# Tile codes for parts of two and three chunks of an edge group, in a one-core graph layer

## What is computed

```python
xn = layernorm(x)
sums   = segment_sum(xn[src], dst)            # 20,000 edges into 625 nodes
counts = segment_sum(1, dst)
gnn = (sums / max(counts, 1)) @ W_l.T + xn @ W_r.T + b_r
x = x + gnn + mixer(xn)                       # 8 heads, second-order attention
h = layernorm(x)
H = gelu(h @ W1 + b1)                         # 1024 wide
e = argmax(H @ Wg + bg)                       # one of 8 experts per node
x = x + prob[e] * (H @ Wd[e] + bd[e])
```

## Time and profile before

| | |
|---|---|
| median of 3 runs | 253.75 us (253.46 to 253.86) |
| the profiled execution: its own time | 254.01 us |
| its span in the profile | 252.3 us |
| TensorE busy | 236.2 us, 94% |
| VectorE busy | 148.1 us, 59% |
| ScalarE busy | 145.2 us, 58% |
| GpSimd busy | 31.8 us, 13% |
| granted TensorE clock | 0.995 of 2.4 GHz |

### The profile page before, as it was taken

The page is one execution under the profiler, slowest core; times in us unless marked ns, Lnnn a source line. Parts: engine busy times, 40 slices in busy tenths (PEclk is TensorE's granted clock), DMA queues, the critical chain, the costliest instruction groups (busy, mean ns, idle before and its releaser), DMA issues.

```text
span 252.3 us, 4726 instructions
## 1 busy us (share of the span) xinstructions
PE 236.2 (94%) x1428; PEld 149.6 (59%) x1429; DVE 148.1 (59%) x422; ACT 145.2 (58%) x223; POOL 31.8 (13%) x64
## 2 busy tenths in 40 slices
PE   7899999998798999999999999998899999999990
PEld 2448675664454553433368886574455578888880
DVE  2999999999999949961125557722800243223220
ACT  2878997999999956899960015444043323333000
POOL 7470000000000008300000000000450000000331
PEclk9999999999999999999999999999999999999997
DMA  6560000000000000099930000030033000000111
GB/s 232 189 216 3 1 3 3 5 4 3 3 5 0 5 3 3 0 370 421 416 130 4 0 0 0 9 131 25 26 84 105 0 1 3 0 1 3 36 34 33
DMA packets 6030, 15.82 MB, mean 63 GB/s; under 512 B 2724, under 2 KB 3783, under 8 KB 4723
## 3 DMA queue, kind: packets, MB, share of 16 engines
q1 hardware_dynamic: 4432, 12.64, 13.5%
q0 software_dynamic: 1280, 1.31, 2.0%
q10 hardware_dynamic: 288, 1.44, 1.4%
HBM read 14.08 MB, written 1.30 MB: 61 GB/s over the span
## 4 chain that ended last, share of the span: by engine, by line
PE 64%; ACT 21%; DVE 11%; issue 1%; POOL 1%; DVEq 0%; POOLq 0%
ACT mem L518 19%; PE ps L1270 16%; PE ps L1208 7%; PE ps L1090 7%; PE ps L1254 6%; PE ps L1111 5%; PE ps L1170 4%; DVE mem L722 4%; PE ps L1238 3%; PE ps L939 3%; DVE mem L725 2%; PE ps L1159 2%; PE ps L1161 2%; PE ps L967 1%; DVE qk_sb L768 1%
## 5 line engine op out<-in xcount | busy, mean ns | idle before, releaser
L518 ACT ACTIVATE mem<-ids_m,half_src 125x628 bf16<-125x628 f16 x96 | 69.7, 814 | 0.0
L722 DVE TENSOR_SCALAR mem<-node_ids,dst_f 125x628 bf16<-125x628 f16 x160 | 53.1, 387 | 0.0
L1004 PE MATMUL ps<-mem 125*128 125x501 bf16 x180 | 50.8, 374 | 0.4 <-issue 0.3
L1270 PE MATMUL ps<-mem 128*125 x192 | 41.6, 379 | 0.0
L1006 PE MATMUL ps<-mem 125*128 125x126 bf16 x180 | 39.3, 219 | 0.0
L1270 PEld LDWEIGHTS ps<-mem 128*125 128x125 f32 x192 | 36.0, 188 | 5.3
L616 ACT ACTIVATE qk_sb<-ps,sc_col 125x626 f32<-125x626 f32 (+1 forms) x40 | 28.6, 778 | 3.7 <-PE ps L1090 3.7
L1004 PEld LDWEIGHTS ps<-mem 125*128 x180 | 17.6, 98 | 20.4 <-issue 1.9
L725 DVE TENSOR_SCALAR mem<-ids_m,src_f 125x628 bf16<-125x628 f16 x64 | 25.0, 390 | 0.0
L665 ACT COPY mem<-mem 128x1000 f32 x8 | 8.2, 1031 | 19.8 <-PE ps L1270 19.8
L1090 PE MATMUL ps<-mem 32*125 32x313 f32 (+1 forms) x160 | 19.1, 472 | 0.2 <-DVE mem L795 0.2
(11 more groups left out here) (204 smaller groups left out, 281.0 us busy)
## 6 DMA issues: line engine op xcount, KB each, us to landing
mem<-in_wd SPq DMA_DIRECT2D x8, 1024.0 KB, 13.1
w_sb<-in_w SPq DMA_DIRECT2D x1, 1024.0 KB, 7.8
vz<-in_bd SPq DMA_DIRECT2D x1, 1000.0 KB
wqkv_sb<-in_w_qkv ACTq DMA_DIRECT2D x1, 768.0 KB, 6.4
x_all<-in_x ACTq DMA_DIRECT2D x1, 640.0 KB, 4.9
row<-rows_sorted SPq DMA_DIRECT2D x1, 579.7 KB
wlr_sb<-in_w_lr SPq DMA_DIRECT2D x1, 512.0 KB, 5.1
bqk_all<-in_b_qk SPq DMA_DIRECT2D x1, 256.0 KB, 4.2
```

Source lines behind the costliest of these rows:

```text
L518: ins = nc.scalar.activation(oh[:, g % OHB, 0, j, :], ids_m1[:, :], ACT.Sign, bias=half_src[:, g * GC + j:g * GC + j + 1])
L722: ins = nc.vector.tensor_scalar(oh[:, g % OHB, 1, j, :], node_ids[:, :], dst_f[:, col:col + 1], None, ALU.is_equal)
L1004: mm(psf[:, bass.ds(tile * BANK, TW + 1)], node_of, oh[:, buf, 0, j, 0:TW + 1], start=False, stop=False, skip_group_check=True)
L1270: ins = mm(ps[0:TP, 4 + n % EB, 0:C], hT_step[:, n % EB, k, :], wd_sb[:, bass.ds(e, 1), k, :], start=(k == 0), stop=(k == KH - 1))
```

## The change

Each group of five chunks gets two codes in place of one, for a part of its first two chunks and a part of the last three. A part's code has six bits: three for the first tile, two for the second tile less one, and one that is set (as the value 4 added to the two bits) for more than two. Four codes, those of a pair's two groups, go into one 24-bit number in float32 on GpSimd, and so into one integer. At a tile border only the part that has the border is repeated at the second tile. For this the sums of the signs are taken by part (weights 1.5 and 1, so that one threshold serves both), the small tables have 64 columns in place of 32, and GpSimd's chain up to `codes_ready` has 20 operations in place of 11. Each part's products have their own tile register and addresses. Two tables move into `mem`.

```diff
+    PARTS = ((0, 2), (2, GC))
+    NS = NG * len(PARTS)
...
-        PAIR = 256
+        PART = 64
+        PAIR = PART ** 4
+        OTHERS = sum((PART - 8) * PART ** s for s in range(4))
...
-            nc.gpsimd.memset(ones_col[:, :], 1.0)
+            nc.gpsimd.memset(part_col[:, 0:1], 1.5)
+            nc.gpsimd.memset(part_col[:, 1:2], 1.0)
...
             step(nc.gpsimd.tensor_tensor(span[:, :], last, first, ALU.subtract))
-            step(nc.gpsimd.tensor_scalar(two_code[:, :], span[:, :], 0.0, 8.0, ALU.is_gt, ALU.mult))
-            step(nc.gpsimd.tensor_scalar(more_code[:, :], span[:, :], 1.0, 128.0, ALU.is_gt, ALU.mult))
-            step(nc.gpsimd.tensor_tensor(two_code[:, :], two_code[:, :], last, ALU.mult))
-            step(nc.gpsimd.tensor_tensor(more_code[:, :], more_code[:, :], first, ALU.add))
+            step(nc.gpsimd.tensor_scalar(more_code[:, :], span[:, :], 1.0, 4.0, ALU.is_gt, ALU.mult))
+            step(nc.gpsimd.tensor_scalar(span[:, :], span[:, :], 0.0, None, ALU.is_gt))
+            step(nc.gpsimd.tensor_scalar(two_code[:, :], last, 2.0, 4.0, ALU.is_lt, ALU.mult))
+            step(nc.gpsimd.tensor_tensor(two_code[:, :], two_code[:, :], last, ALU.add))
+            step(nc.gpsimd.tensor_scalar(two_code[:, :], two_code[:, :], -1.0, None, ALU.add))
+            step(nc.gpsimd.tensor_tensor(two_code[:, :], two_code[:, :], span[:, :], ALU.mult))
             step(nc.gpsimd.tensor_tensor(two_code[:, :], two_code[:, :], more_code[:, :], ALU.add))
-            by_pair = two_code[:, :].rearrange("o (p w) -> o p w", w=2)
-            step(nc.gpsimd.tensor_scalar(pair_hi[:, :], by_pair[:, :, 1], float(PAIR), None, ALU.mult))
-            step(nc.gpsimd.tensor_tensor(pair_hi[:, :], pair_hi[:, :], by_pair[:, :, 0], ALU.add))
-            nc.gpsimd.tensor_copy(flags[:, :], pair_hi[:, :]).then_inc(codes_ready, 1)
+            step(nc.gpsimd.tensor_scalar(two_code[:, :], two_code[:, :], 8.0, None, ALU.mult))
+            step(nc.gpsimd.tensor_tensor(two_code[:, :], two_code[:, :], first, ALU.add))
+            by_pair = two_code[:, :].rearrange("o (p w) -> o p w", w=4)
+            step(nc.gpsimd.tensor_copy(pair_code[:, :], by_pair[:, :, 3]))
+            for s in (2, 1, 0):
+                step(nc.gpsimd.tensor_scalar(pair_code[:, :], pair_code[:, :], float(PART), None, ALU.mult))
+                step(nc.gpsimd.tensor_tensor(pair_code[:, :], pair_code[:, :], by_pair[:, :, s], ALU.add))
+            nc.gpsimd.tensor_copy(flags[:, :], pair_code[:, :]).then_inc(codes_ready, 1)
...
-            for j in range(GC):
-                ins = mm(ps[0:1, 0, 0:(T - 1) * NG], ones_col[:, :], ge[:, :, :, j], start=(j == 0), stop=(j == GC - 1))
+            part_sums = ps[0:1, 0, 0:(T - 1) * NS].rearrange("o (k g s) -> o k g s", k=T - 1, s=len(PARTS))
+            for s, (lo, hi) in enumerate(PARTS):
+                for j in range(lo, hi):
+                    ins = mm(part_sums[:, :, :, s], part_col[:, s:s + 1], ge[:, :, :, j], start=(j == lo),
+                             stop=(j == hi - 1))
...
-            def products(g, tile):
+            def products(g, s, tile):
                 buf = g % OHB
-                for j in range(GC):
+                lo, hi = PARTS[s]
+                for j in range(lo, hi):
...
-            def other_tiles(g, own):
+            def other_tiles(g, s, own):
                 with pe.If(own > 7):
-                    products(g, nc.s_assert_within((own >> 3) & 15, min_val=0, max_val=T - 1,
-                                                   skip_runtime_bounds_check_because="a second tile is there"))
-                    with pe.If(own > 127):
+                    products(g, s, nc.s_assert_within(((own >> 3) & 3) + 1, min_val=1, max_val=T - 1,
+                                                      skip_runtime_bounds_check_because="two bits and one"))
+                    with pe.If(own > 39):
...
             def pair(p):
                 code = codes[p]
-                for g, own in ((2 * p, code), (2 * p + 1, code >> 8)):
-                    first = nc.s_assert_within(own & 7, min_val=0, max_val=T - 1,
-                                               skip_runtime_bounds_check_because="each group has edges, each of a tile")
+                for g in (2 * p, 2 * p + 1):
                     pe.wait_ge(oh_ready, g + 1)
                     pe.wait_ge(steps_ready, g + 1)
-                    products(g, first)
-                with pe.If((code & 0xF8F8) > 0):
-                    other_tiles(2 * p, code & (PAIR - 1))
-                    other_tiles(2 * p + 1, code >> 8)
+                    for s in range(len(PARTS)):
+                        first = nc.s_assert_within((code >> 6 * (2 * (g - 2 * p) + s)) & 7, min_val=0, max_val=T - 1,
+                                                   skip_runtime_bounds_check_because="each part has edges, each of a tile")
+                        products(g, s, first)
+                with pe.If((code & OTHERS) > 0):
+                    for g in (2 * p, 2 * p + 1):
+                        for s in range(len(PARTS)):
+                            other_tiles(g, s, (code >> 6 * (2 * (g - 2 * p) + s)) & (PART - 1))
```

More of the change, by code:

```diff
@@ L83, in gps_layer @@
         BIG = 2 * KH * N
-        assert OH + 6 * N <= WD + BIG and T * (N + 1) <= WD
+        assert OH + 2 * T * NS + 6 * N <= WD + BIG and T * (N + 1) <= WD
         mem = sb("mem", [P, WD + BIG])
@@ L103, in gps_layer @@
         half_src = sb("half_src", [TP, NCH])
-        tile_of = sb("tile_of", [1, T, NG])
-        edge_tiles = sb("edge_tiles", [1, 2, T - 1, NG])
-        between = sb("between", [1, T, NG])
-        span = sb("span", [1, NG])
-        two_code = sb("two_code", [1, NG])
-        more_code = sb("more_code", [1, NG])
-        ones_col = sb("ones_col", [TP, 1], BF16)
-        pair_hi = sb("pair_hi", [1, NP])
+        edge_tiles = sb("edge_tiles", [1, 2, T - 1, NS])
+        span = sb("span", [1, NS])
+        two_code = sb("two_code", [1, NS])
+        more_code = sb("more_code", [1, NS])
+        part_col = sb("part_col", [TP, 2], BF16)
+        pair_code = sb("pair_code", [1, NP])
         flags = sb("flags", [1, NP], I32)
-        more = sb("more", [1, T, NG], I32)
+        more = sb("more", [1, T, NS], I32)
         at_sb = sb("at_sb", [P, T * N])
@@ L116, in gps_layer @@
         qk_sb = sb("qk_sb", [P, T * 4 * QB])
+        tile_of = mem[0:1, OH:OH + T * NS].rearrange("o (t g) -> o t g", t=T)
+        between = mem[0:1, OH + T * NS:OH + 2 * T * NS].rearrange("o (t g) -> o t g", t=T)
         oh = mem[0:TP, 0:OH].bitcast(BF16).rearrange("p (b w j n) -> p b w j n", b=OHB, w=2, j=GC)
@@ L456, in _ @@
             nc.gpsimd.tensor_copy(tri_b[:, :], tri[:, :]).then_inc(consts_ready, 1)
-            step(nc.gpsimd.iota(tile_of[:, :, :], pattern=[[1, T], [0, NG]], base=0, channel_multiplier=0,
+            step(nc.gpsimd.iota(tile_of[:, :, :], pattern=[[1, T], [0, NS]], base=0, channel_multiplier=0,
                                 allow_small_or_imprecise_dtypes=True))
@@ L470, in _ @@
-            by_pair = two_code[:, :].rearrange("o (p w) -> o p w", w=2)
-            step(nc.gpsimd.tensor_scalar(pair_hi[:, :], by_pair[:, :, 1], float(PAIR), None, ALU.mult))
-            step(nc.gpsimd.tensor_tensor(pair_hi[:, :], pair_hi[:, :], by_pair[:, :, 0], ALU.add))
-            nc.gpsimd.tensor_copy(flags[:, :], pair_hi[:, :]).then_inc(codes_ready, 1)
-            step(nc.gpsimd.tensor_tensor(between[:, :, :], tile_of[:, :, :], first[:, None, :].broadcast_to([1, T, NG]),
+            step(nc.gpsimd.tensor_scalar(more_code[:, :], span[:, :], 1.0, 4.0, ALU.is_gt, ALU.mult))
@@ L475, in _ @@
+            nc.gpsimd.tensor_copy(flags[:, :], pair_code[:, :]).then_inc(codes_ready, 1)
+            step(nc.gpsimd.tensor_tensor(between[:, :, :], tile_of[:, :, :], first[:, None, :].broadcast_to([1, T, NS]),
                                          ALU.subtract))
-            step(nc.gpsimd.tensor_tensor(tile_of[:, :, :], last[:, None, :].broadcast_to([1, T, NG]), tile_of[:, :, :],
+            step(nc.gpsimd.tensor_tensor(tile_of[:, :, :], last[:, None, :].broadcast_to([1, T, NS]), tile_of[:, :, :],
@@ L710, in _ @@
             dve.wait_ge(flag_sum, 1)
-            past_first = ps[0:1, 0, 0:(T - 1) * NG].rearrange("p (k g) -> p k g", k=T - 1)
-            nc.vector.tensor_scalar(edge_tiles[:, 0], past_first, GC * TP - 1.0, None, ALU.is_gt)
-            nc.vector.tensor_scalar(edge_tiles[:, 1], past_first, 1.0 - GC * TP, None, ALU.is_gt).then_inc(flag_read, 1)
+            past_first = ps[0:1, 0, 0:(T - 1) * NS].rearrange("p (k g) -> p k g", k=T - 1)
+            nc.vector.tensor_scalar(edge_tiles[:, 0], past_first, 3 * TP - 1.0, None, ALU.is_gt)
+            nc.vector.tensor_scalar(edge_tiles[:, 1], past_first, 1.0 - 3 * TP, None, ALU.is_gt).then_inc(flag_read, 1)
             normalised(1)
@@ L1015, in other_tiles @@
                         with pe.Fori(1, T) as t:
```

(8 more changed lines are left out.)

2 lines of the change are left out of this document (1 added, 1 removed).

## The result

| | before | after |
|---|---|---|
| median, measured side by side | 253.81 us (253.46 to 253.96) | 262.17 us (261.81 to 262.70) |
| ratio, 95% interval | | 1.0331 (1.0310 to 1.0351) |
| span of the profiled execution | 252.3 us | 261.0 us |
| its own time | 254.01 us | 262.70 us |
| granted TensorE clock | 0.995 | 0.997 |

What follows compares the result with a forecast made beforehand. ScalarE's step rows bound the kernel before, TensorE's sequencer after. Closing products at 102.3 instead of 94.9 (late start and dearer pairs, fewer products 0) gave 253.75 + 7.4 = 261.2 us, rounded; range 257.0 to 264.5.

Steps and rivals of the forecast that it cites:

- The late start: TensorE's first pair: its first wait comes at 30.4 us against 28.4, cost 2.0, bounds 1.4 and 3.4.
- the dearer pairs: TensorE's sequencer: pairs without a border go from 3.1 to 3.85 us, those with one from 4.7 to 6.25.
- Part 1: Repeats at tile borders: fewer products spare the array 2.7 us, worth 0 inside ScalarE's unbroken stretch.
- Part 2: GpSimd's longer chain: codes ready at 19.1 us (18.5 to 20.5), delaying loads and pair 0, cost 2.0.
- Part 3: Sequencer's added register work per part: 3.85 us a pair without a border, 6.25 with one.
- the 7.4 of the sum: Forecast total loss in us: closing products at 102.3 instead of 94.9, with nothing behind them cheaper or dearer.
- The rules: Two skill rules weighed, neither in the sum: about 108 ns per compare-and-branch, and GpSimd and VectorE's exclusive port lock.
- the port: Port pair shared by GpSimd and VectorE: longer chain estimated to cost group 2's fills 0.6 us, group 1 gaining 0.4.
- B: Rival: register work hides behind the array, ScalarE stays the bound, only the late start remains; 255.8 to 257.5 us, chance 0.11.
- C: Rival: faster, as GpSimd's wide tables leave group 1's fills on VectorE, which lose 0.6 us; 253.1 us, chance 0.05.
- C's condition: For the faster rival: loads still end before 28.4 us and a pair's issue stays below 4.3.
- E: Rival: array idle in border pairs, so TensorE's granted clock falls to its lower level; about 281 us, chance 0.04.

## Why the prediction was right

**The bound.** Right: ScalarE before, the sequencer after. The late start and the dearer pairs were each measured by themselves.

**Part 1, booked 0.** Right: without any repeats the kernel before is where it was (0.9998).

**Part 2, codes at 19.1 and pair 0 at 30.4.** Measured 19.6 and 30.66. GpSimd's chain begins 0.33 later than it did (wait for VectorE's wider flags, booked at up to 0.3), and its 20 steps take 8.96 us, where the sum has 8.5. Its timeline, first, middle and last operation of the codes and the last of the table (counterpart of the earlier trace rows):

```profile
10.63 0.72 POOL L466 TENSOR_TENSOR edge_tiles<-edge_tiles 1x256 f32<-1x256 f32 x1 [3.56 <-DVE edge_tiles L724]
...
13.51 0.50 POOL L472 TENSOR_SCALAR two_code<-edge_tiles 1x64 f32<-1x64 f32 x1
...
17.01 0.48 POOL L482 TENSOR_SCALAR pair_code<-pair_code 1x16 f32<-1x16 f32 x1
...
19.40 0.19 POOL L484 CAST flags<-pair_code 1x16 int32<-1x16 f32 x1
...
24.61 0.44 POOL L492 CAST more<-mem 1x320 int32<-1x320 f32 x1
```

One-step operations on 16 elements, 0.26 in the earlier trace rows, took up to 0.48: that is the half microsecond. The table was ready at 25.05, as said. The pairs start 30.66 - 28.4 = 2.3 later, predicted 2.0.

**Part 3, 3.85 and 6.25 a pair.** Measured 3.92 and 6.30. The terms were all a little small: 0.3 at the start, 9 x 0.07 and 4 x 0.05 make 1.1, the 1.1 by which the closing products came later than said (103.44 for 102.3). The time moved likewise: 8.4 for the 7.4 of the sum. That 7.4 has a slip: it takes 94.9 for today's closing products, where the line above it has 94.7 (measured 94.68). With 94.7 it would have been 7.6, and the forecast 261.4. Without the border condition a pair takes 3.44, so that condition costs 0.48 a pair and not 0.43. The fused operations are 174, not 170: four more, one for each repeated part.

**What the sequencer can cover.** "In pairs without a border the sequencer is just quick enough; with four that cost 6.25 it isn't." The first half is shown: without the block, and so without borders, ScalarE bounds again. VectorE waited only 0.5 us for `sums` before MA, where I said 1; nothing in the sum hung on it.

**The rules.** For the compare-and-branch the Trainium skill ("Advanced Engine Details and Errata", Control Flow Timing) has about 108 ns; here it was 0.07 to 0.10 where nothing was jumped over, mostly 0.21 to 0.43 otherwise, and up to 2.58. A border pair at 6.30 is above both the 6.25 of the rows and the 6.0 of that figure. The trace's own figure was the better one, and still not the whole price. Of the port, the fills of group 2 take 3.09 us in the changed kernel, 2.05 before, and those of group 1 2.05 for 2.67: 1.0 lost and 0.6 back, where I had estimated 0.6 and 0.4.

**The rivals.** B fell with the changed kernel's 6.3 us pairs and ScalarE's waits. C's gain exists (0.5 us), but the changed kernel pays more for its longer chain on GpSimd, and the loads and pairs broke C's condition. C's 0.6 us for group 1 came out (0.62) partly by luck: its four rows give 0.06 a fill, 0.4 for seven, and the rest is the one fill that was held 0.30. E fell for the changed kernel (its clock stayed at 1.0 from 28 to 106), but the thing itself appeared in the two kernels with longer jumped-over code.

**Left open.** How the 5.1 us of the border block divide between the condition that each pair runs and the four borders was not separated by a run: the kernel meant for it brought its own fetch stalls. The heads of the pairs give a part: from pair 0 to pair 3, where no border is and nothing covers, the changed kernel takes 42.84 - 30.66 = 12.18 us and the one without the block 41.50 - 30.55 = 10.95, so 1.2 are the condition's. For the rest, the condition alone leaves an ordinary pair at 3.9, under ScalarE's 4.54, so the borders should be what decides; that is argued, not shown.

## What to carry to other kernels

Where addresses come out of registers, count the register instructions, waits and branches between two matmuls from the sequencer's rows, and compare a period of that with the period of the engine that bounds: under it they are hidden, over it each is paid, about 0.1 us apiece here. Saving products on an array that waits for another engine gains nothing, and the condition that is written for the saving adds to the sequencer's time in every iteration (0.48 us a pair here). Before moving work into a rarely taken branch, look at how much code will be jumped over.

## What the runs showed of the hardware that I had not expected

- Code that never runs costs time: ten skipped chunk products per pair made the kernel 6.8 us slower. Jumps took up to 2.58 us, where 0.21 to 0.43 is usual, and each one over 0.5 us ended 1.3 to 1.5 us after an instruction packet had landed.
- Stalls of the array of 1.65 to 2.72 us were followed in four cases by products at the lower clock (0.63 in place of 0.38 us for 501 columns), so such a stall can be paid twice; behind others of 1.65 and 1.98 us the granted clock stayed at 1.00.
- A wait more for GpSimd gained 0.5 us: beside its small operations on one partition, seven of VectorE's fills take 2.67 us in place of 2.05, and a single one up to 1.02 in place of 0.37.
